# An earlier guard flag, a last query quarter as two products, and an interleaved second norm in a two-layer kernel on one Trainium2 core

## What is computed

```python
xn = layernorm(x)
x  = x + attn0(xn) + ffn0(xn)      # layer 0
xn = layernorm(x)                  # the "second norm"
x  = x + attn1(xn) + ffn1(xn)      # layer 1

# attn0: a memory M (64 x 128) goes over all 2048 rows
k, q = phi(rmsnorm(xn) @ Wk.T), phi(rmsnorm(xn) @ Wq.T)   # phi(z) = elu(z) + 1
M = ln2(M + eta * |v_t - k_t M| * outer(k_t, v_t))         # for each row t
out = xn + (q @ M_last) @ Wout.T
# ffn0: one expert of two linear layers with a relu
# attn1: rotary embedding on half of the dimensions, causal softmax, 2048 keys
# ffn1: silu gate, two gelu layers of 512, a last layer back to 128
```

## Time and profile before

| | us |
|---|---|
| median of 3 runs | 256.38 |
| lowest, highest | 256.31, 256.75 |
| the profiled execution | 256.91 |
| its span, first to last instruction | 255.1 |
| PE busy | 245.0 (96%) |
| DVE, ACT, POOL busy | 204.5, 185.8, 115.0 |

### The profile page before, as it was taken

The page is one execution under the profiler, slowest core; times in us unless marked ns, Lnnn a source line. Parts: engine busy times, 40 slices in busy tenths (PEclk is TensorE's granted clock), DMA queues, the critical chain, the costliest instruction groups (busy, mean ns, idle before and its releaser), DMA issues.

```text
span 255.1 us, 5149 instructions
## 1 busy us (share of the span) xinstructions
PE 245.0 (96%) x1669; PEld 160.1 (63%) x1673; DVE 204.5 (80%) x681; ACT 185.8 (73%) x460; POOL 115.0 (45%) x150
## 2 busy tenths in 40 slices
PE   7899998999998999999999999999999999999993
PEld 2359554776764477786778767886875444444492
DVE  7888899999958998998899887787613996666674
ACT  2697789976637887887667899989814997777730
POOL 9789700000004589887755994997790000000000
PEclk9999999999999999999999999999999999999999
DMA  6620000000008403000000000000000000000004
GB/s 189 187 81 3 1 0 3 1 0 3 3 3 321 177 15 149 3 1 0 4 0 3 0 0 3 1 1 0 4 3 0 0 0 3 0 1 0 1 29 141
DMA packets 8479, 8.50 MB, mean 33 GB/s; under 512 B 1793, under 2 KB 7554, under 8 KB 7938
## 3 DMA queue, kind: packets, MB, share of 16 engines
q1 hardware_dynamic: 7074, 7.52, 8.8%
q10 hardware_dynamic: 1376, 0.62, 0.9%
HBM read 7.09 MB, written 1.05 MB: 32 GB/s over the span
## 4 chain that ended last, share of the span: by engine, by line
PE 63%; DVE 20%; POOL 6%; ACT 3%; issue 3%; DMA 2%; DVEq 0%; SPq 0%; POOLq 0%; ACTq 0%
PE PS L957 11%; PE PS L956 11%; PE PS L929 8%; PE PS L906 7%; PE PS L919 4%; POOL arena L1497 3%; POOL arena L1498 3%; PE PS L718 3%; DMA x<-L_attn_x 2%; PE PS L672 2%; PE PS L726 2%; DVE mxb L2022 2%; DVE arena L2008 2%; PE PS L575 2%; PE PS L570 2%
## 5 line engine op out<-in xcount | busy, mean ns | idle before, releaser
L956 PE MATMUL PS<-arena 128*128 128x512 f16 x128 | 48.5, 379 | 0.0
L957 PE MATMUL PS<-arena 128*128 128x512 f16 x128 | 48.5, 379 | 0.0
L2080 DVE TENSOR_TENSOR arena<-arena 128x512 f32<-128x512 f32 x32 | 22.2, 693 | 13.0 <-ACT arena L1416 13.0
L906 PE MATMUL PS<-arena 128*128 128x512 f32 (+3 forms) x80 | 31.9, 530 | 0.3 <-ACT arena L1385 0.3
L1415 ACT ACTIVATE arena<-PS,arena 128x512 f32<-128x512 f32 x32 | 22.9, 715 | 9.1 <-PE PS L957 9.1
L1497 POOL TENSOR_TENSOR arena<-arena 128x256 f32<-128x256 f32 x32 | 21.5, 672 | 15.7 <-DVE arena L2014 13.1
L1385 ACT ACTIVATE arena<-PS,lnt 128x512 f32<-128x512 f32 (+3 forms) x40 | 24.8, 628 | 3.2 <-DVE lnt L2029 3.2
L1498 POOL TENSOR_TENSOR arena<-arena,small 128x256 f16<-128x256 f32 (+1 forms) x36 | 23.8, 660 | 2.8
L1505 POOL CAST arena<-arena 128x512 f16<-128x512 f32 x2 | 1.3, 637 | 49.1 <-ACT x L1278 49.1
L1416 ACT ACTIVATE arena<-PS,arena 128x512 f16<-128x512 f32 x32 | 22.8, 712 | 0.0
L2022 DVE TENSOR_REDUCE mxb<-PS 128x1 f32<-128x512 f32 (+3 forms) x40 | 22.1, 601 | 0.0
(11 more groups left out here) (292 smaller groups left out, 614.5 us busy)
## 6 DMA issues: line engine op xcount, KB each, us to landing
arena<-h_T SPq DMA_DIRECT2D x2, 1024.0 KB, 5.9
arena<-cos SPq DMA_DIRECT2D x1, 1024.0 KB, 4.8
arena<-sin SPq DMA_DIRECT2D x1, 1024.0 KB, 6.8
arena<-w_T SPq DMA_DIRECT2D x3, 256.0 KB, 3.1
x<-L_attn_x SPq DMA_DIRECT2D x2, 256.0 KB, 5.5
out<-arena SPq DMA_DIRECT2D x2, 256.0 KB, 2.2
x<-L_attn_x SPq DMA_DIRECT2D x2, 128.0 KB, 2.6
x<-L_attn_x ACTq DMA_DIRECT2D x2, 128.0 KB, 3.2
```

The costliest lines, as they stand in the source:

```text
L906: i = mm(PS[:, k, 0:cnt * P], qT1[:, t * P:(t + 1) * P], kT1[:, c * P:(c + cnt) * P], start=True, stop=not last)
L956: mm(bank(b), wH[:, k, m * P:(m + 1) * P], sH[:, k, cols], start=(k == 0), stop=False)
L957: i = mm(bank(b), wL[:, k, m * P:(m + 1) * P], sL[:, k, cols], start=False, stop=(k == HT4 - 1))
L2080: v.tensor_tensor(RP[m], FP[m], high, ALU.subtract).then_inc(rest_ready, 1)
```

## The change

The tables of cosine and sine get places of their own in the large buffer and are loaded during the scan instead of after it; the rotation's scratch `TURN` moves too. The scan's free slots change: `last_rows` starts at step 16, the copy of `WVO` goes into step 19, the first reciprocal into step 13 and `c0` into step 18 of DVE, the query pieces start a step later, PE's shift of `c0` goes ahead of the last `expert_output`, and the four warming products of step 25 go. After the scan the guard's work stands in front of the rest of the query pieces on DVE and in front of the memory outputs on PE. phi is now formed as min(exp, 1) + relu; for the last quarter of the queries DVE only clamps the exponential (256 columns in one instruction) and PE multiplies both parts with MW and adds them. Eleven warming products around the branch become four. Five instructions that prepare scales move from after the norm to before the tables of the scan on DVE.

In the second norm DVE takes half of the next chunk's statistics before it needs the root of this one; in the last chunk it puts the first two rotary products there. PE transposes tile by tile in the order in which they are normed, and puts the next chunk's transposes between its products. ACT's order changes: copies of transposed tiles earlier, skip copies between the norm's work, the two mask copies before the branch. POOL's key sum waits for DVE's query sum of the same chunk, not for the products.

The diff, cut to its core:

```diff
--- before.py
+++ after.py
+        cosT = Gf[:, S:S + T]
+        sinT = arena[:, at[0]:at[0] + T]
-        TURN = [hBf[:, T * c:T * c + 2 * BANK].rearrange("p (k t) -> p k t", k=2) for c in range(2)]
+        TURN = [hAf[:, 2 * T + 2 * BANK * c:2 * T + 2 * BANK * (c + 1)].rearrange("p (k t) -> p k t", k=2) for c in range(2)]
...
-        LAST_AT = 15
+        LAST_AT = 16
...
-            sp.wait_ge(x1_ready, 2)
-            for i, n in enumerate(("cos", "sin")):
-                sp.dma_start((cosT, sinT)[i], a[n]).then_inc(tab_in, 16)
+            sp.wait_ge(lanes_act, 10)
+            sp.dma_start(cosT, a["cos"]).then_inc(tab_in, 16)
+            sp.wait_ge(tables_ready, 1)
+            sp.wait_ge(terms_act, 2)
+            sp.dma_start(sinT, a["sin"]).then_inc(tab_in, 16)
...
             def memory_output(two, first, end):
                 for k in range(first, end):
-                    pe.wait_ge(q_ready, 2 * (4 * two + k + 1))
+                    pe.wait_ge(q_ready, (11, 13, 13, 13)[k] if two else 2 * (k + 1))
+                    part = slice((4 * two + k) * P, (4 * two + k + 1) * P)
+                    if two and k >= 2:
+                        for c in (2, 3):
+                            h0 = F * (c % 2)
+                            mm(PS[:, c, k * P:(k + 1) * P], QE[h0:h0 + F, part], MW[h0:h0 + F, :], start=False, stop=False)
                     for c in (2 * two, 2 * two + 1):
                         h0 = F * (c % 2)
-                        i = mm(PS[:, c, k * P:(k + 1) * P], QT[h0:h0 + F, (4 * two + k) * P:(4 * two + k + 1) * P], MW[h0:h0 + F, :], start=False, stop=(k == 3))
+                        i = mm(PS[:, c, k * P:(k + 1) * P], QT[h0:h0 + F, part], MW[h0:h0 + F, :], start=False, stop=(k == 3))
                         if k == 3:
                             i.then_inc(ao_done, 1)
-            for j in range(FAR + 1, L):
+            for k, j in enumerate(EO_AT):
                 pe.wait_ge(scan_ready, j + 1)
-                if j in EO_AT:
-                    expert_output(EO_AT.index(j) + 1)
-                elif EO_AT[-1] + 4 < j < L - 2:
-                    keep_warm(4, 4)
+                if j == EO_AT[-1]:
+                    pe.wait_ge(c0_ready, 1)
+                    mm(PS[0:W, 5, HALF:HALF + REST], con[0:W - 1, C_ID + 1:C_ID + 1 + W], c0[0:W - 1, 0:REST], start=True, stop=True).then_inc(shift_done, 1)
+                expert_output(k + 1)
+            pe.wait_ge(wvo_act, 1)
             pe.wait_ge(g_ready, L)
             for twin in range(2):
-                mm(PS[WINDOW * twin:WINDOW * twin + WINDOW, 5, 0:1], SGw[:, :, 1], con[:, C_ID + LAST:C_ID + LAST + 1], start=True, stop=True).then_inc(gcol_done, 1)
+                mm(PS[WINDOW * twin:WINDOW * twin + WINDOW, 7, 2 * D:2 * D + 1], SGw[:, :, 1], con[:, C_ID + LAST:C_ID + LAST + 1], start=True, stop=True).then_inc(gcol_done, 1)
             keep_warm(1, 4)
-            pe.wait_ge(rh_ready, 1)
+            pe.wait_ge(rh_ready, 2)
             mm(PS[:, 6, HALF:HALF + 1], con[:, C_ID + LAST:C_ID + LAST + 1].broadcast_to([P, P]), rh[:, 1:2], start=True, stop=True).then_inc(rhb_done, 1)
-            pe.wait_ge(wvo_act, 1)
+            pe.wait_ge(c0_ready, 2)
+            mm(PS[0:W, 5, HALF + REST:HALF + REST + 1], con[0:W - 1, C_ID + 1:C_ID + 1 + W], c0[0:W - 1, REST:REST + 1], start=True, stop=True).then_inc(shift_done, 1)
+            keep_warm(1, 4)
             pe.wait_ge(uw_ready, 1)
             mm(PS[:, 7, 0:D], UW, VW, start=True, stop=True).then_inc(mw_done, 1)
-            pe.wait_ge(c0_ready, 2)
-            mm(PS[0:W, 5, HALF:HALF + REST + 1], con[0:W - 1, C_ID + 1:C_ID + 1 + W], c0[0:W - 1, :], start=True, stop=True).then_inc(shift_done, 1)
+            keep_warm(1, 4)
+            pe.wait_ge(guard_ready, 2)
+            mm(PS[0:1, 5, 1:2], agree, con[:, C_ONES:C_ONES + 1], start=True, stop=True).then_inc(count_done, 1)
+            keep_warm(1, 4)
             pe.wait_ge(mw_act, 1)
             memory_output(0, 0, 2)
-            pe.wait_ge(agree_ready, 1)
-            mm(PS[0:1, 5, 1:2], agree, con[:, C_ONES:C_ONES + 1], start=True, stop=True).then_inc(count_done, 1)
...
             memory_output(0, 2, 4)
             memory_output(1, 0, 4)
-            keep_warm(4, 4)
+            keep_warm(2, 4)
             general_path(pe, general)
-            keep_warm(7, 4)
+            keep_warm(2, 4)
...
-                pe.wait_ge(xn2_act, 2 * c + 2)
-                pe.wait_ge(xn2_dve, 2 * c + 2)
                 if c >= 2:
                     pe.wait_ge(xt2_act, c - 1)
-                for n in range(4 * c, 4 * c + 4):
+                for k in range(4):
+                    n = 4 * c + (2, 0, 3, 1)[k]
+                    pe.wait_ge(xn2_act if k % 2 else xn2_dve, 2 * c + k // 2 + 1)
                     i = tr(PS[:, b, (n % 4) * P:(n % 4 + 1) * P], xn[:, n, :], ident)
                 i.then_inc(xrt_done, 1)
...
-                if c == 0:
-                    normed(1)
+                if c < 3:
+                    normed(c + 1)
                 if c >= 2:
...
-                for n in ((2,), (3,), (), ())[c]:
-                    normed(n)
...
-                    f(QT[:, cols], bank(Q_BANK[b]), ACT.Copy).then_inc(qphi_act, 1)
+                    f(QT[:, cols], bank(Q_BANK[b]), ACT.Relu, bias=minus_one).then_inc(qphi_act, 1)
...
+                if j == LAST_AT + 3:
+                    act.wait_ge(wvo_done, 1)
+                    f(WVO, PS[:, 7, 0:D], ACT.Copy).then_inc(wvo_act, 1)
...
-            act.wait_ge(wvo_done, 1)
-            f(WVO, PS[:, 7, 0:D], ACT.Copy).then_inc(wvo_act, 1)
             act.wait_ge(rhb_done, 1)
             n = o.did(f(rhb, PS[:, 6, HALF:HALF + 1], ACT.Copy))
             o.need(n)
             act.wait_ge(mw_done, 1)
             f(MW, PS[:, 7, 0:D], ACT.Copy, scale=rhb).then_inc(mw_act, 1)
+            f(ident_b, ident, ACT.Copy).then_inc(mask_act, 1)
+            f(causal_b, con[:, C_CAUSAL:C_CAUSAL + P], ACT.Copy).then_inc(mask_act, 1)
...
+            def skipped(c):
+                b = 4 * ((c + 1) % 2)
+                cols = slice(c * BANK, (c + 1) * BANK)
+                act.wait_ge(skip_done, c + 1)
+                f(qT1[0:ROT, cols], PS[0:ROT, b + 1, :], ACT.Copy).then_inc(skip_act, 1)
+                f(kT1[0:ROT, cols], PS[ROT:P, b + 1, :], ACT.Copy).then_inc(skip_act, 1)
             first_block(1)
             deviations(0)
             first_block(0)
             normed(0)
             first_block(2)
+            transposed(0)
             deviations(1)
-            transposed(0)
+            normed(1)
             first_block(3)
-            normed(1)
             deviations(2)
+            transposed(1)
             normed(2)
-            transposed(1)
             deviations(3)
+            skipped(0)
+            transposed(2)
             normed(3)
-            transposed(2)
+            skipped(1)
+            transposed(3)
             f(small[:, 38:39], lnt[:, 0, 12:13], ACT.Tanh)
-            for c in range(4):
-                b = 4 * ((c + 1) % 2)
-                cols = slice(c * BANK, (c + 1) * BANK)
-                act.wait_ge(skip_done, c + 1)
-                f(qT1[0:ROT, cols], PS[0:ROT, b + 1, :], ACT.Copy).then_inc(skip_act, 1)
-                f(kT1[0:ROT, cols], PS[ROT:P, b + 1, :], ACT.Copy).then_inc(skip_act, 1)
-                if c == 0:
-                    transposed(3)
-                if c == 2:
-                    act.wait_ge(xt2_act, 1)
-                    high(0)
-                    f(ident_b, ident, ACT.Copy).then_inc(mask_act, 1)
-                    f(causal_b, con[:, C_CAUSAL:C_CAUSAL + P], ACT.Copy).then_inc(mask_act, 1)
+            skipped(2)
+            skipped(3)
+            act.wait_ge(xt2_act, 1)
+            high(0)
             act.wait_ge(xt2_act, 4)
...
-                pool.wait_ge(rope_dve, 2 * c + 2)
+                pool.wait_ge(turned_dve, c + 1)
...
+            dve.wait_ge(small_in, 16 * 13)
+            v.tensor_scalar(s1h, s1, 0.5, None, ALU.mult).then_inc(scales_ready, 1)
+            v.scalar_tensor_tensor(out=s12, in0=s1, scalar=0.5, in1=s2, op0=ALU.mult, op1=ALU.mult).then_inc(scales_ready, 1)
+            need(did(v.tensor_tensor(s12a, s1, s2, ALU.mult)))
+            v.tensor_reduce(sums[:, 0:1], s12a, AX.X, ALU.add, apply_absolute_value=True).then_inc(sums_ready, 1)
+            v.tensor_reduce(sums[:, 1:2], sh1, AX.X, ALU.add, apply_absolute_value=True).then_inc(sums_ready, 1)
...
-                    v.scalar_tensor_tensor(out=QT[:, part], in0=QE[:, part], scalar=1.0, in1=QT[:, part], op0=ALU.min, op1=ALU.max).then_inc(q_ready, 1)
+                    v.scalar_tensor_tensor(out=QT[:, part], in0=QE[:, part], scalar=1.0, in1=QT[:, part], op0=ALU.min, op1=ALU.add).then_inc(q_ready, 1)
...
+                    dve.wait_ge(h_ready, REST)
+                    v.reciprocal(rh[:, 0:1], HS[:, REST:REST + 1]).then_inc(rh_ready, 1)
...
-                    if j >= LATENT:
```

(69 more changed lines are left out.)

10 lines of the change are left out of this document (1 added, 9 removed).

## The result

The changed kernel takes 258.17 us (median of five, 257.62 to 258.81) against 256.72 for the kernel before in the same rounds (256.31 to 257.38): ratio 1.0061, 95% interval 1.0035 to 1.0087. Predicted were 254.2 us, range 253.6 to 255.4. The profiled execution took 258.17 with a span of 256.4.

A forecast was written before the change was run, and what follows sets the result against it. TensorE, busy 96% of the span, was taken to bound the kernel by when it gets its work. Engines reach layer 1 2.0 to 2.5 us earlier, taken as -2.2: 256.38 - 2.2 = 254.2 us, range 253.6 to 255.4.

The forecast's parts named there:

- Scan: Layer scan: later last_rows -0.2, early reciprocal +0.1; VectorE's last scan starts 0.1 us earlier.
- Guard: Behind the scan: flag near 72.0, 1.05 us earlier; first statistics near 73.3, also -1.05, bounds -0.6 and -1.2.
- Norm: Second norm: transposes tile by tile, projections from 77.5 for 79.19, -1.7 us, 0.65 more than the flag gave.
- rival 4: Around the flag: TensorE's clock falls with seven warming products gone, projections slow down, 259.4 us; chance 0.04.
- Key sums: Rotation: POOL's sums take 1.15 to 1.27 us, start 0.1 after VectorE's, delay its next by at most 0.1.
- rival 1: Rotation: POOL's key sum takes the full 1.77 us and holds VectorE's next sums, 255.7 us; chance 0.07.
- Values: End of the projections on TensorE: values of layer 1 start at 89.3 for 91.60, -2.3 us.
- Rival 3: Later stage, layer 1: new collisions cost half of the gain, 255.3 us; chance 0.08.

The follow-up runs named there:

- r6: The kernel before with its 16 first warming products halved, so that the code behind stands 32 instructions later: 258.69 us, ratio to before 1.0062.
- r8: The kernel before, in which TensorE alone neither loads the flag nor branches: 256.78 us, ratio to before 0.9996.
- r1: The changed kernel without TensorE's flag load, branch and part of the general path: 255.97 us, ratio to before 0.9969.
- r7: The changed kernel with TensorE's flag load and branch ahead of the last two product columns, general path kept for columns 0 and 1: 255.61 us, ratio 0.9948.
- r0: The changed kernel, unaltered, run again: 257.34 us, ratio to before 1.0033.
- r2: The changed kernel with 64 more instructions in TensorE's general path, which is never run: 259.35 us, ratio to before 1.0100.
- r5: The changed kernel with first warming products cut smaller, so that the code behind stands 24 instructions later: 258.44 us, ratio to before 1.0057.
- r11: r7 with skipped(0) ahead of deviations(3) on ScalarE: 255.38 us, ratio to before 0.9938.
- r10: r7 with the old wait of POOL's key sums, so they start together with VectorE's sums: 255.88 us, ratio to before 0.9960.

## Why the prediction was wrong, step by step

**Scan: two terms right, one not foreseen.** The reciprocal made its stretch 0.08 longer (0.1 predicted), and the step with the late root took 1.25 for 1.43. But the step whose scan starts at 47.19 took 1.41, where the kernel before needs 1.18 for it. It took 1.41 or 1.42 in every trace that has the change, and 1.18 in before, r6 and r8, so it belongs to the change; its cause stays open. From the first scan to the last it is 33.5 us for 33.4, and the last scan is 0.1 late where 0.1 early was predicted.

**Guard: right.** The clamp took 0.29 (0.4 taken, bounds 0.15 to 0.69). Measured from the last scan the flag came 0.97 earlier; 1.05 was predicted, 0.1 of it by the scan.

**Norm: right where TensorE had its instructions.** Without the hole the projections start at 77.32 in r1 and 77.36 in r7; 77.5 was predicted. In these two executions the scan starts 0.37 earlier than in that of before, so the gain is 1.5, where 1.7 was predicted. In after ScalarE's `transposed(0)` had been put ahead of `deviations(1)`, so a late TensorE also held the root and with it VectorE's norm: the 2.07 us. I had seen this order and costed it at 0.25 of idle, on the premise that TensorE is on time.

**The step that failed** is in the norm: "The transposes start tile by tile and only the last one waits: bank 0 copied at 75.5, tiles normed by 76.4, transposed by 76.75". The tiles were normed at 76.95, and the last two transposes started at 78.73, for want of instructions. TensorE's own branch stands in the sum at nothing. I costed the branch on VectorE (load and branch, 1.31 us) and never asked what it does to TensorE, since the trace of before shows no idle time behind it. It shows none because the norm was later than the fetch. The change took away that cover: the transposes came forward from 77.45 to 76.5, and the fetch stood where it was (75.6 in before and r0, 76.4 in after). It also left two warming products of seven behind the target, and moved the target 26 instructions nearer to the boundary. Those five products went into the prediction only as a matter of the clock, under rival 4. They were an edit costed at nothing, and for such an edit the work that hides it has to be named; the fetch behind the branch was that work's other half. The Trainium skill has a rule for such branches in Runtime: NRT & Kernel Launch, Instruction fetch mechanics: program code comes in blocks of 256 instructions, sequentially, and a "taken branch whose target isn't in the current 2-page window forces a DMA fetch of the target page". The runs agree: in r2 and r5 the target lies beyond the next block, and the branch takes 3.40 and 3.82 us. In after the target was still inside, the branch took 0.37, and the stop came 8 instructions later, at the end of the block. I had weighed rules on operations and ports and none on the branch.

**Key sums: right, against rival 1.** Each takes 1.26 to 1.27 and starts 0.1 to 0.15 after VectorE's, and VectorE's next products aren't held.

**Values: the term was too large.** Even without the hole the values start at 89.69 (r1) and 89.73 (r7) for 89.3. I had taken 11.8 us for the four chunks of projections, and they take 12.4 in r1 and r7, with 0.3 of waiting for ScalarE's copy behind `skipped(0)` among them, which r11 takes away. Measured from the start of the scan (0.4 earlier in these two executions) that is 1.5 of gain instead of 2.3: 0.6 by the chunks, 0.2 by the projections' start.

**Rival 3 was there too, small.** Both r1 and r7 lose 0.3 near 115 us (117 in before). VectorE's first cast of a half chunk meets a subtraction on POOL. In before:

```profile
117.04 0.29 DVE L2014 CAST arena<-arena 128x256 f16<-128x256 f32 x1
```

```profile
116.53 0.61 POOL L1498 TENSOR_TENSOR arena<-arena,small 128x256 f16<-128x256 f32 x1
117.28 0.67 POOL L1497 TENSOR_TENSOR arena<-arena 128x256 f32<-128x256 f32 x1
```

and in r7:

```profile
115.40 0.57 DVE L2046 CAST arena<-arena 128x256 f16<-128x256 f32 x1
```

```profile
115.16 0.67 POOL L1509 TENSOR_TENSOR arena<-arena 128x256 f32<-128x256 f32 x1
```

In after the cast takes 0.63, in r1 0.63, in r11, where it starts 0.14 ahead of the same POOL instruction, 0.29. No run was made for this alone; it is read from where the pairs happened to fall. With it the account is: 2.2 predicted; 0.8 too much at the values, 0.3 given back at the cast, which leaves 1.1, and r1 and r7 measured 0.8 and 1.3. The hole takes more than that again: r0 lies 1.4 above r1 in the same rounds, and after, which is 1.45 above the kernel before in its rounds where r7 is 1.3 below it in its own, 2.7 above r7 (r0, 0.58 above the kernel before in its rounds, lies 1.9 above r7).

**Rival 4** had the right mechanism and another cause: the clock fell in the traces of r2, r5 and r6, behind holes that the supply had made, and not in that of after. It is also a part of the result. The mean granted clock was 0.993 in two of the five executions of after (258.72 and 258.81 us, the others 257.62 to 258.17 at 0.998), and 0.992 or 0.993 in four of the twelve of r0 (258.04 to 259.04, the others 256.56 to 257.46 at 0.996 and above). Of the 54 executions of the kernel before beside r0 to r11 one has 0.993 (257.84 us). No trace of these was kept. In r1, r7 and r8 no execution is under 0.995. So the hole cost its own length in every execution, and, it seems, a fall of the clock in about a third of them.

**What stays open.** When a packet is called for is known only roughly. Packets start from 14 instructions ahead of the boundary near 1476 to 90 behind it (1462 in r1, 1491 in r10, 1508 in r7, 1545 in before, 1566 in r6, all counted without regard to how far the engine's queue has run ahead), and no run here tells apart why. Nor is the cause known of the scatter in the hole of one and the same program (1.26 and 1.79), which goes with the start of the packet, 0.8 and 1.2 us behind the branch. What the table does show is that the place decides: eight kernels with the branch, each at a place of its own, two without it, and none out of line.

## What to carry over

A branch over long code that isn't taken isn't free behind its target: count the instructions between the target and the end of what was fetched, and ask whether they last as long as a fetch, 3.4 to 4.1 us here from the branch to the first instruction of the new packet. An idle time that ends with "issue" behind a branch, beside a packet of the instruction queue, was this in all six kernels that showed it. When a change pulls work forward to a branch, or takes filler from behind it, the branch has to move forward too; and since any edit ahead of it shifts its place, a kernel with such a branch should be timed at two or three places before a small difference is put down to anything else.
